# Unread TensorE products, a later last product and other banks for the first expert tile

## What is computed

```python
x = x + tanh(g_xattn[i]) * mixer(ctx, layernorm(x))   # the normalised x is the gate z
x = x + tanh(g_ffn[i]) * ffn(layernorm(x))
# mixer: in-projection, causal convolution of 4 taps, SiLU -> u;
#   x_proj(u) -> dt_lo (16), B (16), C (16); delta = softplus(dt_proj(dt_lo))
#   for each of 16 states n:  s = s * exp(delta * A_n) + delta * u * B_n ;  y += s * C_n
#   y = (y + D * u) * silu(z)
# ffn of layer 0: 16 experts (512 -> 256 -> 512, gated), 4 for each row by grouped top-k, and one shared expert
# ffn of layer 1: base matrix, and LoRA of rank 16 from 8 experts, top 2 by a router
```

## Time and profile before

| | us |
|---|---|
| median of 3 runs | 1559.41 (1557.27 to 1560.66) |
| profiled execution | 1560.78 |
| its span, first to last instruction | 1559.0 |

### The profile page before, as it was taken

The page is one execution under the profiler, slowest core; times in us unless marked ns, Lnnn a source line. Parts: engine busy times, 40 slices in busy tenths (PEclk is TensorE's granted clock), DMA queues, the critical chain, the costliest instruction groups (busy, mean ns, idle before and its releaser), DMA issues.

```text
span 1559.0 us, 13944 instructions
## 1 busy us (share of the span) xinstructions
PE 1263.5 (81%) x4244; PEld 701.1 (45%) x4244; DVE 1413.8 (91%) x1462; ACT 835.8 (54%) x1341; POOL 794.4 (51%) x413
## 2 busy tenths in 40 slices
PE   6785687799699868987869999889998889923888
PEld 2322232343244324442526666566665666612444
DVE  4999999999999999988896999999899999977894
ACT  5754747564765456534864765546655444423442
POOL 0465456545654553350464455655556655565642
PEclk7898899999989988998978999999999999975999
DMA  7354456535553543350465678666887877854531
GB/s 252 96 135 128 106 129 142 140 103 143 140 137 91 146 129 102 91 164 23 94 177 186 237 257 259 234 249 234 268 244 234 280 258 283 267 161 139 164 106 55
DMA packets 99835, 264.27 MB, mean 170 GB/s; under 512 B 10833, under 2 KB 11345, under 8 KB 93617
## 3 DMA queue, kind: packets, MB, share of 16 engines
q1 hardware_dynamic: 87936, 225.36, 49.4%
q0 software_dynamic: 11440, 37.50, 7.2%
q10 hardware_dynamic: 384, 0.52, 0.1%
HBM read 233.73 MB, written 29.62 MB: 169 GB/s over the span
## 4 chain that ended last, share of the span: by engine, by line
DVE 42%; PE 24%; issue 9%; DMA 6%; POOL 5%; ACT 2%; DVEq 0%; SPq 0%; ACTq 0%; POOLq 0%
DVE state L1615 18%; DVE banks L1607 12%; PE banks L1108 8%; PE banks L1119 3%; DMA expert_w<-in_moe_w 3%; PE banks L1018 3%; POOL state L448 2%; DMA ys_d<-expert_out 2%; DVE y_scan L1626 2%; PE banks L1261 2%; PE banks L1067 1%; PE banks L1075 1%; PE banks L1087 1%; DVE du L1331 1%; DVE small L1385 1%
## 5 line engine op out<-in xcount | busy, mean ns | idle before, releaser
L448 POOL TENSOR_TENSOR state<-state,bc_rows 128x1024 f32<-128x1024 f32 x256 | 606.6, 2371 | 659.3 <-DVE banks L1607 659.2
L1018 PE MATMUL banks<-state,ident 128*128 128x512 f32 x640 | 338.1, 660 | 118.2 <-POOL state L448 118.2
L1615 DVE TENSOR_TENSOR_SCAN state<-decay,banks 128x1024 f32<-128x1024 f32 x176 | 402.1, 2285 | 7.0 <-ACT decay L673 1.7
L1607 DVE TENSOR_TENSOR banks<-du,bc_rows 128x1024 f32<-128x1024 f32 x256 | 315.2, 1231 | 12.8 <-issue 0.5
L1108 PE MATMUL banks<-z_gate,expert_w 128*128 128x256 f32 (+1 forms) x1504 | 287.1, 349 | 6.4 <-DMA expert_w<-in_moe_w 5.7
L1108 PEld LDWEIGHTS banks<-z_gate,expert_w 128*128 128x128 f32 x1504 | 251.5, 192 | 61.2 <-issue 21.3
L1018 PEld LDWEIGHTS banks<-state,ident 128*128 128x128 f32 x640 | 121.3, 204 | 307.9 <-POOL state L448 194.4
L673 ACT ACTIVATE decay<-delta,neg_a 128x511 f32<-128x511 f32 x352 | 230.7, 712 | 53.9 <-DVE state L1615 45.9
L1615 DVE TENSOR_TENSOR_SCAN state<-expert_w,banks 128x1024 f32<-128x1024 f32 x80 | 182.9, 2286 | 6.8 <-ACT expert_w L673 4.2
L1119 PE MATMUL banks<-expert_w,hidden 128*128 128x512 f32 x316 | 156.9, 612 | 2.9 <-DVE hidden L1636 2.9
L1626 DVE TENSOR_TENSOR y_scan<-y_scan,state 128x1024 f32<-128x1024 f32 x96 | 118.4, 1234 | 3.3 <-POOL state L448 3.3
(11 more groups left out here) (303 smaller groups left out, 1590.5 us busy)
## 6 DMA issues: line engine op xcount, KB each, us to landing
bc_rows<-bc_d SPq DMA_DIRECT2D x208, 512.0 KB, 5.0
expert_w<-in_moe_w SPq DMA_DIRECT2D x48, 1536.0 KB, 9.0
ys_d<-expert_out SPq DMA_DIRECT2D x32, 512.0 KB, 10.2
...
```

Source lines behind the costliest of these rows:

```text
L448: nc.gpsimd.tensor_tensor(W[:, c % 4], W[:, c % 4], bcast2(BC[:, u, 1, :]), ALU.mult).then_inc(mulc_done, 1)
L1018: mm = nc.tensor.matmul(PS[:, m], ID[:, :], W[:, c % 4, m, :], start=False, stop=True, skip_group_check=True)
L1607: nc.vector.tensor_tensor(drive(s), DU[:, s % 2, 2 * h:2 * h + 2, :], bcast2(BC[:, u, 0, :]), ALU.mult).then_inc(mulb_done, 1)
L1615: nc.vector.tensor_tensor_scan(flat(W[:, c % 4]), flat(DAS[c % da_slots(s, i)]), flat(drive(s)), 0.0, ALU.mult, ALU.add).then_inc(scan_don ...
```

## The change

- The product at the end of stages 0 to 3 waits for the next stage's first `mul_b`, as all others do. That of stage four still doesn't.
- Tile 0 is transposed into banks 4 and 5 and has its gate and up products there (`XT(j)`, `GU(j, it)`), the other tiles as before. Its transposes stand behind the sum of unit 5 of the last turn, ScalarE's `tile_rows(0, h)` ahead of stage 5's first decay. The waits for `y4_ready` and for stage four's scans stand behind tile 0's `tile_in`. GpSimd gathers tile 0 after unit 3 (before: 4) and tile 1 after unit 7 (before: 6).
- `stay_warm(bank, n)` makes `n` products of the 128 x 128 identity with a 128 x 128 block of ones into a bank that nobody reads before it is written anew: 4, 4, 4 and 3 in `x_proj(0)`; 7 after each sum of units 1 to 4, 6 and 7 of stage four's last turn; 24 ahead of the tail's first `y_transposes`, once three of the first sequence's four row blocks are combined; 14 ahead of each `row_transposes`.

```diff
--- before.py
+++ after.py
@@ -150,7 +150,9 @@
         INDEX = PRE[1][:, 0:NCH]
         MIDL = [bank[:, 0:2 * MR].rearrange("p (q m) -> p q m", m=MR) for bank in (PRE[0], AUX[0])]
-        XT = PS[:, 0:2].rearrange("p a (k r) -> p a k r", k=ET // 2)
+
+        XT = lambda j: (PS[:, 0:2] if j else PS[:, 4:6]).rearrange("p a (k r) -> p a k r", k=ET // 2)
+        GU = lambda j, it: PS[:, it if j else 4 + it]
         bc_d = nc.dram_tensor("bc_d", (STAGES, 2 * NS, L), F32, kind="Internal").ap()
@@ -441,7 +443,7 @@
                 k = HS * s + i * HPT + c
                 pool.wait_ge(scan_done, k + 1 + PRE_SCAN)
                 routed = s == NB - 1 and i == TURNS - 1 and c == 5 or s == NB and k + 1 == HS * NB + 2 * HPT
-                if (k + 1) % HS and not routed:
+                if ((k + 1) % HS or s < NB) and not routed:
                     pool.wait_ge(mulb_done, k + 2)
                 u = place(s, i, c)[2]
@@ -467,11 +469,11 @@
             for i in range(TURNS):
                 for c in range(HPT):
                     mul_c(NB, i, c)
-                    if i == 3 and c == 4:
+                    if i == 3 and c == 3:
                         pool.wait_ge(xn_stored, 16 * NB)
                         pool.wait_ge(index_ready, 1)
                         gather_rows(0)
-                    if i == 3 and c == 6:
+                    if i == 3 and c == 7:
                         pool.wait_ge(shgu_done, IT * NB)
                         gather_rows(1)
             for s in range(FIRST_B, STAGES):
@@ -720,14 +722,14 @@
                 if j:
                     act.wait_ge(gu_done, j * 2)
                 n = P * BLOCKS[j]
-                nc.scalar.activation(XST[:, 2 * h:2 * h + 2, 0:n], XT[:, h, :, 0:n], ACT.Copy).then_inc(xst_ready, 1)
+                nc.scalar.activation(XST[:, 2 * h:2 * h + 2, 0:n], XT(j)[:, h, :, 0:n], ACT.Copy).then_inc(xst_ready, 1)
             def tile_tanh(j, it):
                 act.wait_ge(gu_done, j * 2 + it + 1)
                 if j >= 2:
                     act.wait_ge(y_done, DONE[j - 1])
                 n = P * BLOCKS[j]
-                nc.scalar.activation(HT[:, j % 2, it, 0:n], PS[:, it, 0:n], ACT.Tanh, scale=0.5).then_inc(sil_ready, 1)
+                nc.scalar.activation(HT[:, j % 2, it, 0:n], GU(j, it)[:, 0:n], ACT.Tanh, scale=0.5).then_inc(sil_ready, 1)
             def tile_out(j):
                 if j:
@@ -851,6 +853,8 @@
                 if c == 6:
                     step_log(p)
             seed(p)
+            for h in range(2):
+                tile_rows(0, h)
             def tile_turn(s, i, prep):
@@ -883,7 +887,7 @@
                             plus_half(p, 0)
                     if j >= 0:
                         tile_tanh(j, 1)
-                    if j < NTILE - 1:
+                    if 0 <= j < NTILE - 1:
                         tile_rows(j + 1, 0)
                     if prep:
                         if n in (8, 9):
@@ -972,6 +976,11 @@
                                           start=False, stop=True, skip_group_check=True)
                 mm.then_inc(conv_done, 1)
+            def stay_warm(bank, n):
+
+                for _ in range(n):
+                    nc.tensor.matmul(bank[:, 0:P], ID[:, :], ON[:, :], start=True, stop=True)
+
             def x_proj(s):
                 if s:
@@ -984,8 +993,12 @@
                     pe.wait_ge(u_ready, ET * s + et + 1)
                     mm = nc.tensor.matmul(PRE[0][0:DR + 2 * NS, :], XPW[:, lay(s), et, :], DU[:, s % 2, et, :],
                                           start=(et == 0), stop=(et == ET - 1))
+                    if s == 0 and et < ET - 1:
+                        stay_warm(AUX[1], 4)
                 if et == ET - 1:
                     mm.then_inc(xproj_done, 1)
+                    if s == 0:
+                        stay_warm(AUX[1], 3)
             def dt_proj(s, pair):
                 for et in (2 * pair, 2 * pair + 1):
@@ -1084,7 +1097,7 @@
                 for k in range(2):
                     for r in range(BLOCKS[j]):
                         at = (2 * h + k) * P
-                        mm = nc.tensor.transpose(XT[:, h, k, r * P:(r + 1) * P], rows_of(j)[:, r, at:at + P], ID[:, :])
+                        mm = nc.tensor.transpose(XT(j)[:, h, k, r * P:(r + 1) * P], rows_of(j)[:, r, at:at + P], ID[:, :])
                 mm.then_inc(xt_done, 1)
             def index_round(n):
@@ -1105,7 +1118,7 @@
                     for g in range(2):
                         for k in range(ET):
                             at = g * WGU + k * INNER + it * P
-                            mm = nc.tensor.matmul(PS[:, it, g * TILE:g * TILE + n], MW[:, u % 2, at:at + P],
+                            mm = nc.tensor.matmul(GU(j, it)[:, g * TILE:g * TILE + n], MW[:, u % 2, at:at + P],
                                                   XST[:, k, 0:n], start=(k == 0), stop=(k == ET - 1))
                     mm.then_inc(gu_done, 1)
@@ -1220,10 +1233,17 @@
                 sum_state(s, 3, c)
                 if c == 0:
                     index_round(ROUNDS - 1)
-            pe.wait_ge(y4_ready, 1)
-            pe.wait_ge(scan_done, HS * FIRST_B + PRE_SCAN)
-            for h in range(2):
-                tile_transposes(0, h)
+                if c == 1:
+                    pe.wait_ge(dt_read, ET * (FIRST_B + 1))
+                if 1 <= c < 5:
+                    stay_warm(PRE[0], 7)
+                if c == 5:
+                    pe.wait_ge(index_ready, 1)
+                    for h in range(2):
+                        tile_transposes(0, h)
+                if c >= 6:
+                    pe.wait_ge(xst_ready, 2)
+                    stay_warm(PRE[0], 7)
             def tile_turn(s, i, prep):
                 p = s + 1
@@ -1233,6 +1253,10 @@
                     if j < 0:
                         continue
                     tile_in(j)
+                    if j == 0:
+
+                        pe.wait_ge(y4_ready, 1)
+                        pe.wait_ge(scan_done, HS * FIRST_B + PRE_SCAN)
                     for it in range(IT):
                         if j < NTILE - 1:
                             tile_transposes(j + 1, it)
@@ -1274,6 +1298,9 @@
                     for q in range(QT):
                         mm = nc.tensor.transpose(PRE[1][:, q * P:(q + 1) * P], MID[:, q, :], ID[:, :])
                     mm.then_inc(midt_done, 1)
+                if b == 0:
+                    pe.wait_ge(combined, TOPK * (QT - 1))
+                    stay_warm(PRE[1], 24)
                 if b < NB:
                     y_transposes(f, Y[:, b], (0, 1))
                     y_transposes(f, Y[:, b], (2, 3))
@@ -1283,6 +1310,7 @@
                         nc.tensor.matmul(PS[:, q], MIDT[:, q * P:(q + 1) * P], LB, start=False, stop=True,
                                          skip_group_check=True).then_inc(ffn_done, 1)
                 if b < NB:
+                    stay_warm(PRE[1], 14)
                     xnt = XNT1[b % 2]
                     row_transposes(f, XN1[b % 2])
                     for q in range(QT):
@@ -1630,10 +1658,10 @@
                 n = P * BLOCKS[j]
                 h = HT[:, j % 2, it, 0:n]
                 dve.wait_ge(sil_ready, j * 2 + it + 1)
-                nc.vector.scalar_tensor_tensor(out=h, in0=h, scalar=1.0, in1=PS[:, it, 0:n], op0=ALU.add,
+                nc.vector.scalar_tensor_tensor(out=h, in0=h, scalar=1.0, in1=GU(j, it)[:, 0:n], op0=ALU.add,
                                                op1=ALU.mult).then_inc(hg_ready, 1)
                 dve.wait_ge(hg_ready, j * 2 + it + 1)
-                nc.vector.tensor_tensor(h, h, PS[:, it, TILE:TILE + n], ALU.mult).then_inc(h_ready, 1)
+                nc.vector.tensor_tensor(h, h, GU(j, it)[:, TILE:TILE + n], ALU.mult).then_inc(h_ready, 1)
             def shared_hidden(b, it):
```

## The result

| | before | after |
|---|---|---|
| median, us | 1558.34 (1556.07 to 1560.66) | 1538.06 (1536.87 to 1538.37) |
| profiled execution, us | 1560.78 | 1536.87 |
| its span | 1559.0 | 1535.1 |
| mean TensorE clock | 0.922 | 0.948 |

The ratio is 0.9863, with a 95% interval from 0.9847 to 0.9879: 20.3 us saved by the medians, 23.9 between the two profiled executions. The forecast was 1537.4 us. In a later comparison on another chip the same kernel had 0.9881 (0.9853 to 0.9908).

A forecast was written before the change was run, and what follows sets the result against it. VectorE's own list, busy 91% of the span, was taken to set the pace. Gains 3.9 + 8.6 + 7.1 + 2.4 = 22.0 us, from 1559.4, gave 1537.4 us by the median; forecast 1534 to 1541 (0.6), range 1532 to 1547.

The forecast's parts named there:

- Part 2: At the ends of stages 0 to 3, `delta_u` no longer runs beside GpSimd's last product: gain 8.6 us, bounds 0 to 8.6.
- The term 2.15 an end: `delta_u` takes 3.37 us beside GpSimd's product and 1.22 with GpSimd idle: 2.15 saved at each of four stage ends.
- rival (b): At the stage ends, VectorE runs into TensorE's convolutions or ScalarE's work behind them; half gone 1541.7 us, all 1546; chance 0.1.
- signs of being wrong: Clock drops inside filled stretches, a new wait at VectorE's first units of stages 1 to 4, or tile stages lengthen.
- the cover: At the first stage end, `sum_skip` could start at 193.2 against 195.31 today: 2.0 us left before TensorE's lateness reaches VectorE.
- Part 3: End of stage four: the 9.5 us wait at tile 0's first hidden step goes, less 2.35: gain 7.1, bounds 3.5 to 9.5.
- rival c: Unread products leave the clock unchanged, the product meets VectorE elsewhere; only the new banks remain, worth 3.5: 1556 us; chance 0.03.
- Part 1: Head: unread products hold the clock through `x_proj` and `dt_proj`, so `step_abs` ends earlier: gain 3.9 us, bounds -0.8 to 3.9.
- from there to the first scan it is a chain: Head, behind `step_abs`: ScalarE and VectorE work up to the first scan moves as a whole, keeping the 3.9 us gain.
- Part 4: Tail: unread products raise the clock; 1.35 us in batch 0, 0.4 in batch 2, 0.6 in batch 3: 2.4, bounds -1 to 4.
- (a): Clock isn't held in the head or stage four; loses 4.7 and 3.6, one alone 1541 to 1542, both 1545.7; chance 0.2.
- (d): Slower: unread products run at half clock throughout; head +5, stage four +9, batch 3 +4, less 8.6: 1569 us; chance 0.04.

The follow-up runs named there:

- the banks alone: Kernel before with only tile 0's new banks and its transposes and copies moved ahead; no unread products, GpSimd's old order: 1552.01 us, ratio 0.9947.
- ends_alone: Kernel before with one edit, the last product's wait for the next `mul_b` at the four stage ends: 1548.69 us, ratio 0.9933.
- stage4_no_unread: Changed kernel without the unread products of stage four; its banks and order stay: 1542.41 us, ratio 0.9885.
- order_back: Changed kernel with GpSimd's gathers in stage four's last turn back where they stood before: 1540.99 us, ratio 0.9891.
- tail_bare: Changed kernel without any unread products in the tail, neither the 24 nor the 14s: 1541.46 us, ratio 0.9893.
- all_four: Changed kernel with nine unread products in stage zero, later 24, 22 for batch 0's 14, last transposes earlier, GpSimd's old stage-four order: 1542.17 us, ratio 0.9896.

## Why the prediction was right

**The sum** was 22.0 between profiled executions, where 23.9 came, and 1537.4 by the median, where 1538.06 came. By time, the stage ends alone (10.5) and the banks alone (8.3) make 18.8, and the whole change in its second comparison 18.6; each of the three has an interval of 3 us or more to either side. Two of the four parts carry the sum, the stage ends and stage four. The other two are within the noise of the time and smaller in the rows than forecast: 0.4 to 1.3 at 70 us instead of 3.9, and about 1.4 instead of 2.4 in the tail. That the total came out all the same is partly luck. Against the forecast the profiled execution has 0.9 less in the head and 1.7 less in stage 0, and 0.8 more in stages 0 to 3, 1.4 more at stage four, 1.7 more in the tile stages (2.5 of it the wait at 1040) and 0.6 more in the tail: errors of both signs, which make 1.9 together.

**Part 2 (8.6)** was right and is shown by itself: 9.6. The term 2.15 an end came out at 2.16 or 2.17. The give-back that rival (b) feared is real but small (1.7 at the third end) and lies on its ScalarE side: there, ahead of the seed and the gate, ScalarE's tanh waits 4.82 us for TensorE's shared-expert products (at 450.30 in the changed kernel), and it comes and goes with the clock, as told above. It is a new wait at VectorE's first unit of a stage, one of the signs of being wrong that the prediction named. The convolutions behind the sum did no harm, with the cover used up: `sum_skip` started at 191.80, straight behind them, and VectorE was 1.3 us ahead of before by then, so that this is 193.1 in the time of before, where the prediction had 193.2. In ends_alone it started at 193.25, 0.21 us after VectorE's gating.

**Part 3 (7.1)** came out at 8.5. The stall went wholly and the contention was 2.16 (4.63 for 2.47), as the sum had it. The gathers' new place, booked at 0.2, cost next to nothing: 0.7 at a sum step (2.05 us instead of 1.34), with 0.6 back at a `mul_b` (1.84 us before, 1.23 now). Most of the rest of the 1.4 are shorter waits at the next steps of tile 0 and 1. But its bounds were wrong: half clock was to leave 3.5, and stage4_no_unread, where the clock came back ahead of tile 0, has 7.1; the banks by themselves were to be worth 3.5 (rival c), and are worth 8.3 in the execution that has them. The step that failed is that I added a late product, a half clock and an occupied bank as if each kept its share whatever became of the others. The Trainium skill, page "SBUF — State Buffer", section "Who interferes with whom", has VectorE and GpSimd shut each other out, and I wrote that the sum would be 2.15 better without that. The rows agree with the rule (2.47 against 4.61 to 4.64 in each execution), but not with my use of it: order_back avoids the meeting and is 1.4 worse, as its product comes later by more than the meeting costs.

**Part 1 (3.9)** was mis-sized twice. The head gave 3.0 in that execution, but 2.1 of it comes without the unread products too, if the first transfers are a little later; I took the fall of the clock at 21.7 (by the 0.67 of the earlier trace rows it was at 21.3) for a property of the kernel, where the traces have it in two of five heads without unread products. And "from there to the first scan it is a chain" stopped too early: the eighth scan waits for a decay that stands behind two SiLU steps, which wait for TensorE's convolutions, and there 1.7 are given back. Net of both, 1.3 are left at 70 us in the first execution of the change and 0.4 in the second.

**Part 4 (2.4)** has the right sum by one pair of executions (2.6 to 2.8 against tail_bare), and 1.4 by the means of all; there luck is in it. The shares were wrong: against tail_bare batch 0, which was to give 1.35, gives nothing, batch 2 gives 1.2 instead of 0.4 and batch 3 1.8 instead of 0.6. That the 24 cost nothing was right; they also bought nothing in the changed kernel (the first transposes took 1.97).

**Rivals.** (a), the clock isn't held, did not occur in either profiled execution of the change, in the head or in stage four; its price in stage four was 1.4 in the one execution without the products, not 3.6. (b) occurred in part. (c) had a wrong price. (d) was far off: in stage four the products ran at full clock, except once in all_four, where seven of them took 1.3 us longer.
